# When a cross-attention and feed-forward kernel issues its query projections and its odd output projections

## What is computed

```python
x = x + xattn(layernorm(x), ctx, ctx, Wq, Wk, Wv, Wfc, bfc)
#   q = xn @ Wq.T; k, v = ctx @ Wk.T, ctx @ Wv.T
#   out = softmax(q @ k.T / 4) @ v;  out @ Wfc.T + bfc
x = x + ffn(layernorm(x))
#   (gelu(x8 @ w_gating[0]) * (x8 @ w_gating[1]))8 @ w_linear
```

## Time and profile before

| what | value |
|---|---|
| median of 3 runs | 466.07 us (465.42 to 466.16) |
| the profiled execution | 465.95 us |
| its span, first to last instruction | 463.8 us |
| TensorE busy | 430.3 us, 93% |
| VectorE, ScalarE, GpSimd busy | 72%, 67%, 51% |
| chain that ended last, by engine | PE 62%, DVE 11%, issue 8%, POOL 8%, ACT 7% |

### The profile page before, as it was taken

One profiled execution on the slowest core, in us unless ns is written; L12 is line 12 of the kernel. 1 busy time (PEld: TensorE's weight loads), 2 busy tenths in 40 slices (PEclk: granted clock), 3 DMA queues, 4 the chain that ended last, 5 costly groups with the idle time before them and its releaser, 6 DMA issues.

```text
span 463.8 us, 11802 instructions
## 1 busy us (share of the span) xinstructions
PE 430.3 (93%) x4620; PEld 346.0 (75%) x4620; DVE 334.6 (72%) x704; ACT 313.0 (67%) x578; POOL 236.4 (51%) x226
## 2 busy tenths in 40 slices
PE   7867969889999999999999999999999999899997
PEld 6746848767787877877787878877787878558973
DVE  4776587976897579966897579966897579575542
ACT  6848784987379745977379745977379744885541
POOL 5577982695228713684228813684228812492000
PEclk9967799999999999999999999999999999999999
DMA  7797769264602560045401551035401251000001
GB/s 286 283 255 287 230 182 294 79 206 133 161 3 56 152 136 28 3 98 152 116 4 37 152 142 39 3 94 156 118 3 42 76 126 37 3 24 24 3 25 45
DMA packets 21239, 49.79 MB, mean 107 GB/s; under 512 B 4672, under 2 KB 5184, under 8 KB 21184
## 3 DMA queue, kind: packets, MB, share of 16 engines
q1 hardware_dynamic: 20862, 48.24, 36.2%
q10 hardware_dynamic: 322, 0.80, 0.7%
HBM read 23.86 MB, written 4.19 MB: 60 GB/s over the span
## 4 chain that ended last, share of the span: by engine, by line
PE 62%; DVE 11%; issue 8%; POOL 8%; ACT 7%; DMA 2%; ACTq 1%; POOLq 0%; SPq 0%; DVEq 0%
PE bank L644 16%; PE bank L664 10%; PE bank L443 6%; PE bank L445 6%; PE bank L444 6%; PE bank L551 5%; POOL plo L1297 5%; PE bank L518 4%; DVE mneg L1081 4%; PE bank L478 3%; PE bank L569 2%; PE bank L571 2%; ACT phi L840 1%; DMA qs<-cq 1%; DVE prod L1146 1%
## 5 line engine op out<-in xcount | busy, mean ns | idle before, releaser
L1297 POOL TENSOR_TENSOR plo<-p,phi 128x512 f16<-128x512 f32 x128 | 149.8, 1181 | 60.9 <-ACT phi L840 59.9
L644 PE MATMUL bank<-x2T,wgate 128*128 128x128 fp8e4 x2048 | 131.3, 221 | 3.6 <-DVE xr L1159 3.2
L644 PEld LDWEIGHTS bank<-x2T,wgate 128*128 128x128 fp8e4 x2048 | 117.0, 99 | 19.2 <-issue 12.1
L837 ACT ACTIVATE p<-bank 128x512 f32<-128x512 f32 x128 | 77.6, 606 | 20.0 <-PE bank L551 19.6
L1081 DVE TENSOR_REDUCE mneg<-bank 128x4 fp32r<-128x512 f32 x128 | 84.4, 684 | 7.6 <-PE bank L518 7.2
L840 ACT ACTIVATE phi<-bank 128x512 f16<-128x512 f32 x128 | 77.4, 605 | 0.0
L664 PE MATMUL bank<-wlin,act 128*128 128x512 fp8e4 x256 | 72.4, 378 | 0.0
L859 ACT ACTIVATE gate<-bank 128x512 bf16<-128x512 f32 x64 | 38.2, 597 | 50.1 <-PE bank L644 37.3
L863 ACT CAST ff<-bank 128x512 bf16<-128x512 f32 x64 | 37.5, 587 | 49.3 <-PE bank L644 49.3
L518 PE MATMUL bank<-kmask,cq 128*128 128x512 f32 x128 | 58.1, 480 | 4.5 <-DVE mneg L1081 2.8
L551 PE MATMUL bank<-qs,ks 98*128 98x512 f32 x128 | 55.5, 434 | 5.1 <-ACT phi L840 2.5
(11 more groups left out here) (117 smaller groups left out, 813.2 us busy)
## 6 DMA issues: line engine op xcount, KB each, us to landing
qs<-cq SPq DMA_DIRECT2D x90, 128.0 KB, 2.5
stage<-in_w SPq DMA_DIRECT2D x14, 512.0 KB, 5.4
ks<-khl SPq DMA_DIRECT2D x96, 64.0 KB, 2.0
cin<-in_ctx SPq DMA_DIRECT2D x8, 512.0 KB, 4.4
xr<-in_x SPq DMA_DIRECT2D x16, 256.0 KB, 4.5
out<-xr SPq DMA_DIRECT2D x16, 256.0 KB, 2.7
xr<-in_w SPq DMA_DIRECT2D x6, 512.0 KB, 6.2
raw_g<-in_w SPq DMA_DIRECT2D x4, 512.0 KB, 5.9
```

Of the source, the lines that this page charges most:

```text
L644: mm = pe.matmul(out[:, h * SEQ:(h + 1) * SEQ], wgate8[:, UH * v + h, kk, part, :], x2T[:, b % NB, kk, :], start=kk == 0, stop=kk == KT - 1)
L837: act.activation(p32[:, e % P32BUF, :], T[n % 2][:, :], ACT.Exp, scale=QUARTER).then_inc(p32_ok, 1)
L1297: pool.tensor_tensor(plo[:, e % PBUF, :], p32[:, e % P32BUF, :], phi[:, e % PBUF, :], ALU.subtract).then_inc(plo_ok, 1)
```

## The change

Two tables change, and nothing else. In phases 1 to 6 each of the four heads of a query projection is issued whole in slots 8, 10, 12 and 14, where it was issued in halves in slots 8 to 15; in phase 0 whole in 7, 9, 11 and 13, where it was in halves in 7 to 14. The bank after j = 1 is complete one slot earlier (10 for 11, in phase 0 9 for 10), the one after j = 3 as well (14 for 15, 13 for 14); `queries_hi` and `queries_lo` follow the table. In phases 1 to 7 the output projection of the odd batch goes two steps in slot 4 and two in slot 6, where it went one step in each of 4, 5, 6 and 7; its residual and its rstd are in slot 7 in place of 8, the normalisation in slot 9 in place of 10. `turn2` stays at 13.

```diff
-S_Q = {True: tuple(range(7, 15)), False: tuple(range(8, 16))}
+S_Q = {True: (7, 7, 9, 9, 11, 11, 13, 13), False: (8, 8, 10, 10, 12, 12, 14, 14)}
 ...
 CHAIN_E = {True: dict(turn=13, project=(14, 14, 15, 15), residual=16, rstd=16, norm=16, turn2=18),
-           False: dict(turn=0, project=(4, 5, 6, 7), residual=8, rstd=8, norm=9, turn2=13)}
+           False: dict(turn=0, project=(4, 4, 6, 6), residual=7, rstd=7, norm=8, turn2=13)}
```

## The result

The changed kernel takes 474.92 us (median of 4 runs, 473.65 to 477.3) against 466.12 (4 runs, 465.42 to 468.26): ratio 1.0187, with a 95% interval of 1.0133 to 1.0241. The forecast was 474.4, in a range of 471.2 to 478.0. The profiled execution took 474.22 us, 8.27 more than that of before. A ratio leaves out runs counted as slow (over 1.5% above the fastest of the same kernel), so it can differ a little from the quotient of the medians.

The account below looks back on a forecast made before the run. TensorE, busy 93% of the span, was taken to set the pace. Terms 7.0 + 0.75 + 0 + 0.3 + 0.25 = 8.3 us on the profiled 465.95 give 474.25, put at 474.4 for the median; range 471.2 to 478.0.

Parts of the forecast that it names:

- The residual ahead of xT_low: VectorE's slot 7, phases 2 to 6: residual's wait delays xT_low, stalling TensorE's queries 1.4 us a phase, 7.0 in all.
- the forecast's 1.3 to 1.5: Sign in TensorE's timeline: a gap of 1.3 to 1.5 us before the first query matmul in phases 2 to 6.
- Fewer seams: TensorE's fp8 to fp32 matmul changes are free: 0, bound 8.0 us saved; rival with real seams and stall, 466.4, chance 0.06.
- Short slots: Slots 9 and 11 shrink to about 0.9 us; nothing starves in phases 2 to 6: 0, at most 0.3 a slot.
- The end of the slots: Before the units: queries_lo leaves VectorE's last stretch, out_lo comes later, nearly cancelling: +0.15 us a phase, +0.75 in five.
- Phase 1: The stall of about 1.75 us replaces later waiting for GpSimd there: term 0, bounds 0 and +1.8.
- a rival for phases 2 to 6: Clock falls: each 1.4 us pause brings TensorE to half its clock, 8.3 us more, 482.7 in all; chance 0.04.
- Phase 7: Last slots run at GpSimd's pace; later slot 7 and earlier rstd put that chain back: +0.25 us, bounds 0 and +0.7.
- phase 0: First heavy slot delays ScalarE, which feeds the transposed attention output TensorE waits for: +0.3 us, bounds -0.7 and +1.5.
- a sign that such pauses are harmless: Evidence against the clock falling: phase 7's pause of 1.14 us, with short ones around it, leaves the clock at 1.00.

Follow-up runs that it names:

- The swap: Changed kernel with the second xT_low ahead of the residual in VectorE's slot 7, residual still in slot 7: 468.37 us, ratio 1.0026.
- the residual moved alone: Kernel of before with only the odd batch's residual moved from slot 8 to 7, output projection still in slots 4 to 7: 483.2 us.
- the chain alone: Kernel of before with only the odd output projection 2 + 2 in slots 4 and 6 and its residual in 7: 472.62 us, ratio 1.0117.
- finish first: Kernel of before with finish ahead of the first maxima in VectorE's slot 17: 461.45 us against 465.88, ratio 0.991.
- the first four experiments: Changed kernel with residual back in slot 8 (468.7 us) or xT_low ahead of it (468.37); kernel of before with whole queries only (468.91) or odd projection and residual only (472.62).

## Why the prediction was right

**The residual ahead of xT_low (7.0 us predicted).** Right in place, kind and size. 1.43 us a phase where 1.4 was worked out, 7.15 in five. Each step of the sum is in the rows: the end of the projection at 13.25 us into the phase (by the forecast 201.20 - 187.98 = 13.22), the residual 0.11 later, four operations in 1.82, xT_low done 2.41 after the residual began. The swap shows that this order is the cause, and the residual moved alone that the size follows from what is waited for. The gap that the trace prints is 1.26 and just under the forecast's 1.3 to 1.5: the printed gap is idle time behind the modelled end of the last matmul, while the delay is the distance between starts.

**Fewer seams (0).** Right. The slots take 29.94 us with the projection alone and 30.08 with the queries alone, for 29.96.

**Short slots (0).** Right for phases 2 to 6, by the same two kernels.

**The end of the slots (+0.15 a phase).** Right; 0.12 was measured with the queries alone. The forecast called this two shifts that cancel nearly. The traces bear it out. In phase 2 with the residual back in slot 8, `scores_t` of slot 15 starts 0.67 us later than before (25.77 into the phase against 25.10), and from there to the units takes 4.32 us for 4.87.

**Phase 1 (0, up to +1.8).** Absorbed, as argued, where the clock stays up; +1.08 in the first trace by a stretch at half the clock. The forecast had this mechanism as a rival for phases 2 to 6. It did not happen there in any of the three traces with the gap of 1.26, nor in the one with 2.13. In phase 1 it happened in one of two traces of the changed kernel, and not behind the same pause of 2.0 in the kernel with the chain alone, nor behind 2.13 with the residual moved alone. So whether this pause brought the clock down in the one trace isn't shown.

**Phase 7 (+0.25) and phase 0 (+0.3).** Phase 7 gave +0.24. The forecast put it down to a later slot 7 and an earlier rstd; the projection alone gives all of it, so the rstd adds nothing. Phase 0's slots gave -0.19 in the first trace. Phase 0 scatters too much to tell: slots and units together took 53.2 and 52.9 us in the two traces of before, 52.7 and 53.4 in those of the changed kernel, and up to 56.3 in others that leave phase 0 alone. Whether whole heads cost anything there stays open, and the medians give a hint that stays unexplained. Take from each kernel's distance to before what phases 2 to 6 and the 0.24 of phase 7 explain. The five kernels with whole heads are left 0.8 to 1.6 us above, the two with half heads (the chain alone, finish first) 1.5 below. Most intervals are about 1.5 us either way, so none tells much alone, but the signs all agree. The traces don't confirm it: phases 0 and 1 together average 107.2 us in the six with whole heads and 107.4 in the six with halves.

The total of 8.3 is the sum that was worked out, but agreement so close is luck. Phase 1 was 1.08 us over its term of 0, and phase 0, whole, came to 52.7 for 53.2, 0.8 under its term of +0.3. The two nearly cancel.

## What to carry to other kernels

Where an engine's queue is written by hand, look at each operation that waits and ask who is waiting for what stands behind it. Moving an operation one slot ahead so that its own result comes sooner can put its wait in front of something that the bottleneck engine needs at once; here that cost 1.43 us in each of five phases. The cure is to let the urgent and ready one go first, and the same look at the end of the slots, at `finish` behind the maxima, gave 0.9% on the kernel of before (0.6 to 1.2% by the interval). Fewer changes between fp8 and fp32 matmuls were worth nothing here, where the starts showed no gap: compare distances between starts, not the length of one record.

## What was not expected of the hardware

In phase 7 TensorE pauses for 1.14 us and then 0.45 in the trace of before, with the clock full; the forecast took that as a sign that such pauses are harmless. In the kernel with the queries alone, whose phase 7 is the same, pauses of 1.19 and 0.45 were followed by half the clock:

```profile
401.59 0.47 PE L551 MATMUL bank<-qs,ks 98*128 98x512 f32 x1 [1.19 <-ACT phi L840]
402.96 0.70 PE L551 MATMUL bank<-qs,ks 98*128 98x512 f32 x1 [0.45 <-ACT phi L840]
```
```profile
401.50:403.10 1.60, 1.06 (x4) 0.44 (x4) 0.69 (x1) 1.60 (x4) 1.28 (x2) 1.00 0.00 0
403.10:406.50 3.40, 3.40 (x24) 1.97 (x24) 0.56 (x2) 2.97 (x7) 3.28 (x3) 0.50 0.00 0
```

Its phase 7 took 24.84 us for 23.29. Two more traces had this in phase 7: the residual moved alone, after pauses of 1.14 and 0.45, and finish first on the changed kernel, after 1.15 and 0.45. The other nine traces show the same two pauses, 1.14 to 1.16 and 0.45 or 0.46, and the full clock.

Half the clock also came at the start of phase 1 in three traces, those whose first `scores_t` there waited longest for a DMA: 3.00 us (queries alone), 2.41 (residual moved alone) and 1.85 (the swap). In the other nine that wait was 1.44 us or less, and the clock stayed full.

So one trace without a drop does not clear a pause. Part of the scatter between executions of one kernel goes with the clock: of the 23 runs of before that stand beside the first four experiments, the fastest, 462.69 us, has a mean granted clock of 0.989, and the five longest, 468.36 to 468.96, have 0.974 to 0.980.
